# Inverse norms of q and k: a clamp and a power on GpSimd in place of VectorE's clamp and ScalarE's logarithm and exponential

## The reference

```
q, k, v = split(shift_tokens(x) @ Wqkv[i])        # 16 heads of 64 each
q = q / maximum(norm(q), 1e-12) * q_scale          # per token and head
k = k / maximum(norm(k), 1e-12) * k_scale
q = q*cos*scale + rotate_half(q)*sin*scale         # rotary; k with 1/scale
attn = softmax(8 * q @ k.T, within 32-token windows and the window before)
x = attn @ v @ Wo[i] + x
x = gated feed-forward(shift_tokens(x)) + x
```

## Time and profile before

| | |
|---|---|
| median of 3 runs | 4265.62 us (4262.28 to 4284.45) |
| the profiled execution, own time | 4266.14 us |
| its span | 4264.4 us, 141285 instructions |
| PE busy | 3242.7 us (76%) |
| DVE busy | 3305.7 us (78%) |
| ACT busy | 2288.3 us (54%) |
| POOL busy | 2656.3 us (62%) |
| mean granted clock of PE | 0.905 of full |

### The profile page before, as it was taken

One profiled execution on the slowest core, in us unless ns is written; L12 is line 12 of the kernel. 1 busy time (PEld: TensorE's weight loads), 2 busy tenths in 40 slices (PEclk: granted clock), 3 DMA queues, 4 the chain that ended last, 5 costly groups with the idle time before them and its releaser, 6 DMA issues. The chain is left out here.

```text
span 4264.4 us, 141285 instructions
## 1 busy us (share of the span) xinstructions
PE 3242.7 (76%) x60012; PEld 2436.0 (57%) x60398; DVE 3305.7 (78%) x4029; ACT 2288.3 (54%) x4574; POOL 2656.3 (62%) x2014
## 2 busy tenths in 40 slices
PE   3020201898989899988989898989889998989895
PEld 2020201666666666666666666666666666666663
DVE  4969696877787777777777777777877777777774
ACT  2010101666666666666666666566666666666664
POOL 2848484766666666666666666666666666666662
PEclk9565655999999999999999999999999999999998
DMA  0000002111011101111111111111111110111112
GB/s 24 0 7 0 7 0 63 35 30 30 28 30 55 30 29 30 30 31 53 31 30 30 31 53 30 30 30 30 54 30 30 30 30 28 55 28 30 29 30 67
DMA packets 92063, 133.70 MB, mean 31 GB/s; under 512 B 20761, under 2 KB 42032, under 8 KB 90544
## 3 DMA queue, kind: packets, MB, share of 16 engines
q1 hardware_dynamic: 84490, 122.09, 9.7%
q10 hardware_dynamic: 6950, 2.39, 0.2%
HBM read 25.60 MB, written 4.46 MB: 7 GB/s over the span
## 5 line engine op out<-in xcount | busy, mean ns | idle before, releaser
L978 POOL TENSOR_TENSOR qs<-rprod 128x512 f32<-128x512 f32 x768 | 993.6, 1303 | 850.5 <-DVE rprod L1048 835.5
L1048 DVE TENSOR_TENSOR rprod<-ps,tab 128x1024 f32<-128x1024 f32 x768 | 923.5, 1220 | 406.7 <-PE ps L735 318.3
L989 POOL TENSOR_TENSOR qs<-qs,rr 128x512 f32<-128x512 f32 x768 | 805.8, 1070 | 277.3 <-ACT rr L920 273.9
L733 PE MATMUL ps<-wh,xls 128*128 128x512 f32 x1152 | 588.4, 511 | 47.8 <-PEq L689 42.0
L784 PE MATMUL ps<-pt,v 64*64 64x32 f32 x24768 | 443.8, 221 | 185.4 <-ACT pt L910 182.1
L784 PEld LDWEIGHTS ps<-pt,v 64*64 64x64 f32 x24768 | 399.9, 135 | 263.8 <-ACT pt L910 228.7
L744 PE MATMUL ps<-con,qs 128*128 128x128 f32 x3080 | 513.5, 290 | 0.1
L994 POOL TENSOR_TENSOR pr<-pr,rinv 128x512 f32<-128x512 f32 x386 | 403.1, 1044 | 123.9 <-DVE rinv L1090 123.4
L898 ACT ACTIVATE sq<-ps 128x512 f32<-128x512 f32 x384 | 228.3, 595 | 446.7 <-PE ps L735 441.9
L763 PE MATMUL ps<-kT,qT 64*32 64x64 f32 x24704 | 423.7, 218 | 57.4 <-ACT gx L965 0.7
L1066 DVE TENSOR_REDUCE ssq<-sq 128x16 f32<-128x1024 f32 x384 | 464.0, 1208 | 0.0
(11 more groups left out here) (159 smaller groups left out, 6002.7 us busy)
## 6 DMA issues: line engine op xcount, KB each, us to landing
v<-v SPq DMA_DIRECT2D x384, 192.0 KB
v<-v SPq DMA_DIRECT2D x288, 64.0 KB
raw<-in_L_ffn_Wqkv SPq DMA_DIRECT2D x7, 1536.0 KB, 6.6
wo<-in_L_ffn_Wo SPq DMA_DIRECT2D x6, 512.0 KB, 8.1
sT<-so ACTq DMA_DIRECT2D x3, 768.0 KB, 3.3
xnat<-in_L_attn_hidden_states SPq DMA_DIRECT2D x8, 256.0 KB, 3.5
srow<-sT SPq DMA_DIRECT2D x8, 256.0 KB, 3.3
xrow<-in_L_attn_hidden_states SPq DMA_DIRECT2D x8, 256.0 KB, 4.0
```

Of the source, the lines that this page charges most:

```text
L733: nc.tensor.matmul(dst, al, bh, start=True, stop=False)
L978: nc.gpsimd.tensor_tensor(qs[:, i % 2, j].rearrange("p (h s d) -> p h s d", s=2, d=HALF), prod[:, 0, j].rearrange("p (h s d) -> p h s d", ...
L989: nc.gpsimd.tensor_tensor(q3, q3, rr[:, 8 * j:8 * j + 8].unsqueeze(2).broadcast_to([P, 8, DH]), ALU.mult).then_inc(cur["mul"], 1)
L1048: return nc.vector.tensor_tensor(prod[:, :, j, :].rearrange("p c (h d) -> p c h d", d=DH), ps[:, bank, :].rearrange("p (h d) -> p h d", d= ...
```

## The change

DVE's clamp and ACT's `Ln` and `Exp` are taken away. POOL gets, between its rotary sums and its multiplications by `rr`, a clamp of the 128x16 sums (`tensor_scalar`, maximum) and a power (`tensor_tensor` with `ALU.pow`, whose second operand is a tile of -0.5, set once). The power waits for the clamp on a semaphore. The factor `RN` that `Ln` took back goes into the scale of ACT's two squares. DVE's sum of squares now waits for the `rr` of the step before. Nothing else is moved.

```
@@ set-up
+    nhalf = sb("nhalf", [P, 16])
-            nc.vector.memset(eps[:], EPS).then_inc(s_lo, 1)
+            nc.vector.memset(eps[:], EPS)
+            nc.vector.memset(nhalf[:], -0.5).then_inc(s_lo, 1)
@@ scalar
-  nc.scalar.activation(sq[:, 1, :], ps[:, BB, :], ACT.Square).then_inc(cur["sqk"], 1)
+  nc.scalar.activation(sq[:, 1, :], ps[:, BB, :], ACT.Square, scale=RN).then_inc(cur["sqk"], 1)
...
-  nc.scalar.activation(sq[:, 0, :], ps[:, A, :], ACT.Square).then_inc(cur["sqq"], 1)
+  nc.scalar.activation(sq[:, 0, :], ps[:, A, :], ACT.Square, scale=RN).then_inc(cur["sqq"], 1)
...
-  if full:
-      act.wait_ge(cur["g"], i + 1)
-      nc.scalar.activation(gs[:], gs[:], ACT.Ln, scale=RN * RN).then_inc(cur["ln"], 1)
-      act.wait_ge(cur["ln"], i + 1)
-      after(act, "mul", 2 * i)
-      nc.scalar.activation(rr[:], gs[:], ACT.Exp, scale=-0.5).then_inc(cur["r"], 1)
@@ gpsimd
+  pool.wait_ge(cur["ss"], i + 1)
+  after(pool, "mul", 2 * i)
+  nc.gpsimd.tensor_scalar(gs[:], ssq[:], 1e-24 * RN * RN, None, ALU.max).then_inc(cur["g"], 1)
+  pool.wait_ge(cur["g"], i + 1)
+  nc.gpsimd.tensor_tensor(rr[:], gs[:], nhalf[:], ALU.pow).then_inc(cur["r"], 1)
   pool.wait_ge(cur["r"], i + 1)
@@ vector
   dve.wait_ge(cur["sqq"], i + 1)
+  after(dve, "r", i)
   nc.vector.tensor_reduce(ssq[:], sq[:].rearrange("p a (h d) -> p (a h) d", d=DH), AX_X,
                           ALU.add).then_inc(cur["ss"], 1)
-  dve.wait_ge(cur["ss"], i + 1)
-  after(dve, "r", i)
-  nc.vector.tensor_scalar(gs[:], ssq[:], 1e-24, None, ALU.max).then_inc(cur["g"], 1)
```

## The result

The changed kernel takes 4562.94 us (median of four runs, 4558.44 to 4567.65) against 4263.95 us for the kernel before (four runs): a ratio of 1.0695, 95% interval 1.0662 to 1.0728. The forecast was 4230 us, and the time lies outside the range too (up to 4420). What came is rival A, POOL late behind a long power, and worse than A was priced.

The account below looks back on a forecast made before the run. No engine was full; PE and DVE wait for each other in turn. Step terms summed to 0.61 us a round, 29 us over 48 rounds, giving 4236.6 us, rounded down to 4230; range 4175 to 4420.

Parts of the forecast that it names:

- rival A: POOL's power delays the softmax multiplication; PE waits in step 4, then five more steps: 4423 us at 2.8 us; chance 0.28.
- I take 0.9 (25 steps): POOL's power on 16 columns, absent from the trace: estimated as 0.1 + 0.032 k us for k steps, taken as 0.9 us.
- break-even of 2.3 us: Power length on POOL at which PE's loss from the late softmax multiplication equals the gain of 0.61 us a round.
- Where the two meet: DVE instructions lengthened beside POOL's work: step 5 keeps 0.05 of 0.34 us, step 4 loses 0.05.
- 6.8 us in a step of some 9: not full: POOL's own list per step after the change: 2.50 + 2.04 + 1.04 + 1.2 us, leaving room.
- Reduction to maximum: On DVE, start of the sum of squares to start of the softmax maximum without the clamp: 1.14 us in every step.
- step 0: DVE without the clamp starts the maximum earlier, from 1.39 us after the reduction to 1.14: gain 0.25 us.
- step 5: DVE freed 0.34 us; the split beside POOL's later softmax multiplication leaves 0.05 us, ends 0 and 0.34.
- Step 4: DVE's copy lengthens beside POOL's later softmax multiplication: -0.05 us a round, ends -0.35 and +0.25.
- step 7: DVE without the clamp starts the maximum earlier, passed on over `fl` to PE's up projection: gain 0.19 us.
- Step 6: DVE's 0.34 us, travelling over ACT's list to the square of k, counted for half the rounds: gain 0.17 us.
- Rival B: DVE's freed time ends in contention and PE's rounds: 0.26 us a round, 12 us, 4253 us; chance 0.17.

Follow-up runs that it names:

- experiment 2: The changed kernel with the power on 8 of 16 columns only, the k half of `rr` set to a constant: 4340.53 us, ratio 1.0187.
- experiment 5: The kernel before, without ACT's `Ln` and `Exp`; DVE's clamp becomes maximum and product in one instruction, power left out: 4270.09 us against 4262.64.
- experiment 4: The kernel before, without DVE's clamp; `Ln` reads the sums with the bound as bias, POOL gets nothing: 4244.77 us, ratio 0.9953.
- experiment 1: The changed kernel with a product by a constant in place of the power: 4220.07 us against 4262.56, ratio 0.9892.
- experiment 3: The changed kernel, full computation, with POOL's softmax multiplication ahead of the two multiplications by `rr`: 4313.34 us, ratio 1.0123.
- experiment 7: The changed kernel with the power on 8 columns and the split moved to steps 1 (ACT) and 2 (DVE): 4234.73 us, ratio 0.9928.
- experiment 10: The changed kernel with the power on 8 columns and the softmax multiplication ahead of the multiplications by `rr`: 4316.82 us against 4274.09, ratio 1.0102.
- experiment 12: The changed kernel, full power, softmax multiplication ahead, split moved to steps 1 (ACT) and 2 (DVE): 4306.12 us against 4274.09, ratio 1.0079.
- experiment 6: The changed kernel with a product for the power, split moved from steps 3 (ACT) and 5 (DVE) to 1 and 2: 4098.71 us, ratio 0.9609.
- experiment 8: The kernel before without DVE's clamp (bound in `Ln`'s bias), split moved to steps 1 (ACT) and 2 (DVE): 4122.63 us against 4269.79.

## Why the prediction was wrong

**The step that failed: "I take 0.9 (25 steps)".** The power takes 2.93 us. The three sizes, 1.037, 1.666 and 2.929 us at 4, 8 and 16 columns, lie on one line: (1.666 - 1.037) / 4 = 0.157 and (2.929 - 1.666) / 8 = 0.158 us a column, and 0.40 us that don't depend on the columns. The estimate had the form right, but at the assumed 25 steps of 2 ns it has 0.05 us a column; the measured slope is that of 79 such steps, and the fixed part is four times the 0.1 us. The text said itself that no row bounded the power from above, and then chose a value in the lower part; its own line for 100 steps (3.3 us) was nearer. With such a term the price decides the sign, and the value from between the ends was a guess. The estimate of 1.6 us, thirty assumed steps at a figure of the Trainium skill (GPSIMD Engine Reference, Performance pitfalls for Q7 kernels), was too low as well. What the prediction hung on it, a gain of still some 30 us, is refuted by experiment 2: with 1.67 us `fl` did run at 0.74 us, and the kernel lost 78.

**Rival A had the place and the order right and the size wrong.** Put into its formula, a power of 2.93 us and the clamp's 0.25 give d = 0.14 + 2.03 + 0.10 = 2.27, a loss of 1.41 + 5 x 0.77 - 0.61 = 4.65 us a round: 4489 us. Measured were 4563. Its break-even of 2.3 us is refuted more plainly: it lies between 1.04 us (44 us faster) and 1.67 us (78 us slower). Two things were missing. One is contention, which the prediction's section "Where the two meet" placed rightly in steps 4 and 5 but sized too small (-0.05 and 0.05): at a power of 1.04 us the copies and the split take 0.83 us a round more than before, at 1.67 us 1.68 us more. The Trainium skill's rule (GPSIMD Engine Reference, Key points) is that GpSimd shares its SBUF interfaces with VectorE and contends with instructions that have two SBUF inputs or run in a 2-port perf mode. The longer split, with two inputs, agrees with it (0.69 to 1.44 us). The copies, which have one input, were held up as well (0.42 to 1.17 us); in which mode they ran, no run here shows. The other is POOL's own list: "6.8 us in a step of some 9: not full" becomes 8.71 us, and then lateness often no longer dies out within a step: in 208 of 384 steps POOL begins its sums without a pause (3 before). In the timeline after, POOL's sums themselves end late, 1.3 us after the reduction in step 4 where 0.3 was assumed. Nor do "five more steps" pay alike: it is steps 1, 4 and 6.

**What held.** Reduction to maximum: 1.13 us against 1.14. Without the power step 0 gains 0.28 us (0.25 forecast) and step 5 0.36, the whole of the 0.34 of which contention was to leave 0.05. Step 4 gained 0.13 (a loss of 0.05 was booked), step 7 0.18 (0.19). Step 6 gained 0.04 (0.17 booked), so the half-count there was generous. The sum without the power is 0.99 us a round, where the prediction had said 1.0 for a short power; that it fits so well is luck, as step 4 makes up for step 6. Taking away ACT's two instructions gained nothing (experiment 5). The clamp took 0.25 us (0.15 forecast). Rival B, freed time that ends in contention, fits experiment 4 (18 us with a longer `fl`, where experiment 1 has 42), but was not isolated there.

**What stays open.** Of the 343 us that the power costs, order alone gives back 250 (experiment 3), but that can't be called the share of lateness: the same exchange at 8 columns gives 35 of 120 (78 less 43 above before), and lateness and contention seem to replace one another (experiment 7). How the 343 us divide between the three causes isn't settled; that each of them acts, lateness, contention and a full POOL, is shown by experiments 3, 10 and 12 in turn. Why step 6 passed on so little of DVE's 0.34 us was not tried.

## What to carry to other kernels

An operation of unknown price on a path with a margin is a bet on the price: before choosing a value, work out from which price on the change loses, and give the chance to that. An engine at 62% of the span can have less than one instruction of room in each step: compare its list with the shortest step, and ask which instructions of other engines its displaced work will lie on. And look for the step where the engine waits anyway: moving the split of the next input from a step where DVE runs without a pause into one where it waited 2.55 us was worth some 120 us (experiments 6 and 8), more than anything done to the norms; where POOL was full, it brought 19 (experiment 12).

## What the runs showed of the hardware that was not expected

- A power of fp32 on POOL costs 0.40 us + 0.158 us a column on 128 partitions (4, 8 and 16 columns); a product of the same 16 columns 0.22 us, a maximum with a constant 0.25 us.
- POOL's multiplication holds up DVE's copies of 64x512 fp32, which have one input, from 0.42 to 1.31 us; the second half of the split goes from 0.69 to 1.44 and `fl` from 0.74 to 1.47 (experiment 4). The pair on POOL is held up too, 2.04 to 2.94 us. Beside POOL's power of 2.93 us `fl` takes 0.74 us.
- `Ln` with its bias from a tile takes 310 ns, without 218 ns.
